# A gated two-layer transformer block on one Trainium2 core: the gathers, the row addition and the order of the last pass

## The reference

```python
def reference(x, ctx_1024, fside, g_xattn, g_ffn, ...):
    x = x + jnp.tanh(g_xattn[0]) * _L0_xattn_ref(_layernorm(x), ctx_1024, ctx_1024, ...)   # mLSTM heads
    x = x + jnp.tanh(g_ffn[0]) * _L0_ffn_ref(_layernorm(x), wg, w1, b1, w2, b2)            # 8 experts
    x = x + jnp.tanh(g_xattn[1]) * _L1_xattn_ref(_layernorm(x), ctx_1024, ctx_1024, fside, W1, b1, W2, b2)
    x = x + jnp.tanh(g_ffn[1]) * _L1_ffn_ref(_layernorm(x), CB, SCB, bias)
    return x

def _L1_xattn_ref(q, k, v1, mask, W1, b1, W2, b2):
    qp = _proj(q, W1, b1, W2, b2)                 # two linear maps
    kp = _proj(k, W1, b1, W2, b2)
    qk = jnp.einsum('bqd,bkd->bqk', qp, kp) * scale + mask
    return jnp.einsum('bqk,bkd->bqd', jax.nn.softmax(qk, axis=-1), v1)

def _L1_ffn_ref(x, CB, SCB, bias):
    return jnp.einsum('bsk,nk->bsn', x, CB) * (SCB * (1.0 / 127.0)) + bias
```

## Time and profile before

| | |
|---|---|
| median of 3 runs | 575.7 us (573.4 to 580.27) |
| profiled execution | 577.31 us, of which the span of the engines' work is 575.5 us |
| last pass in it | first gather at 421.54 us, end at 575.5 us |
| busy share of the span | PE 83%, DVE 58%, ACT 53%, POOL 38% |

### The profile page before, as it was taken

How to read it: one execution, slowest core, us unless ns; L and a number is a source line. 1 busy time by engine, 2 the same in 40 slices (tenths; PEclk the granted TensorE clock), 3 DMA queues, 4 the chain that set the end, 5 groups by cost and what they waited for, 6 DMA issues and landing times. The chain is left out here.

```text
span 575.5 us, 12773 instructions
## 1 busy us (share of the span) xinstructions
PE 478.4 (83%) x3787; PEld 358.4 (62%) x3787; DVE 333.2 (58%) x1455; ACT 306.5 (53%) x764; POOL 217.1 (38%) x210
## 2 busy tenths in 40 slices
PE   3589999999999999964469999999905788888884
PEld 2567787887877778843327777777702455665652
DVE  6335778877778777796322223333213667788772
ACT  4667666656566656331123333333204678888872
POOL 4301124434444435456500000000058888888400
PEclk9997778777787777795569999999965999999997
DMA  4973112222222111141122443343142556666531
GB/s 120 211 197 92 57 57 75 76 75 74 74 75 74 55 54 38 29 122 37 38 55 56 110 111 110 110 109 93 38 113 34 111 109 145 142 137 139 132 93 36
DMA packets 85067, 51.98 MB, mean 90 GB/s; under 512 B 7555, under 2 KB 78886, under 8 KB 85030
## 3 DMA queue, kind: packets, MB, share of 16 engines
q1 hardware_dynamic: 73766, 43.09, 27.3%
q0 software_dynamic: 11264, 8.43, 8.6%
HBM read 26.07 MB, written 16.91 MB: 75 GB/s over the span
## 5 line engine op out<-in xcount | busy, mean ns | idle before, releaser
L684 POOL DMA_INDIRECT s_xs<-slots_y,s_gidx x64 | 98.8, 1544 | 153.8 <-DMA slots_y<-s_ye 134.6
L814 ACT ACTIVATE s_ht<-heads,s_cols 128x512 f32<-128x512 f32 x64 | 44.0, 687 | 85.0 <-PE heads L1061 84.7
L147 ACT ACTIVATE s_xn<-s_xs,s_ln_shift,s_ln_rstd 128x128 f32 (+1 forms) x192 | 77.6, 481 | 15.6 <-DVE s_ln_shift L140 15.5
L662 POOL DMA_INDIRECT slots_x<-s_xn,s_sidx x64 | 62.8, 982 | 22.9 <-issue 22.9
L99 DVE BATCH_NORM_STATS2 s_ln_stats<-s_xs 128x6 f32 (+1 forms) x256 | 54.5, 279 | 25.8 <-DMA s_xs<-slots_y,s_gidx 20.3
L1061 PE MATMUL heads<-s_xet,s_w_sb 128*128 128x512 f32 x128 | 60.2, 615 | 1.7 <-DVE s_xet L1433 1.7
L1068 PE MATMUL bank<-s_w_sb,s_ht 128*128 128x128 f32 x512 | 59.9, 276 | 0.9 <-DVE s_ye L1442 0.9
L1068 PEld LDWEIGHTS bank<-s_w_sb,s_ht 128*128 128x128 f32 x512 | 58.5, 192 | 1.5 <-issue 1.5
L648 POOL TENSOR_TENSOR s_hs<-s_hs,s_head_w 128x512 f32<-128x512 f32 x16 | 20.3, 1268 | 95.0 <-DVE s_hs L1314 94.9
L960 PE MATMUL heads<-s_dec_r,s_dec_l 128*128 128x512 f32 x64 | 50.6, 938 | 2.0 <-DMA s_dec_r<-s_mrow 2.0
L985 PE MATMUL heads<-s_vaug,s_cw 64*64 64x33 f32 x1024 | 50.1, 270 | 0.1
(11 more groups left out here) (190 smaller groups left out, 934.5 us busy)
## 6 DMA issues: line engine op xcount, KB each, us to landing
slots_x<-s_xe SPq DMA_DIRECT2D x8, 516.0 KB, 8.2
s_xe<-slots_x SPq DMA_DIRECT2D x16, 258.0 KB, 3.0
s_xs<-in_x_dram SPq DMA_DIRECT2D x16, 256.0 KB, 3.0
s_ctxb<-in_ctx_dram SPq DMA_DIRECT2D x16, 256.0 KB, 3.2
s_kpt<-s_kt SPq DMA_DIRECT2D x16, 256.0 KB, 2.8
s_w_sb<-in_L_ffn_w_dram SPq DMA_DIRECT2D x16, 256.0 KB, 3.2
slots_y<-s_ye SPq DMA_DIRECT2D x16, 256.0 KB, 2.3
s_ctxv<-in_ctx_dram SPq DMA_DIRECT2D x16, 256.0 KB, 3.7
```

Of the source, the lines that this page charges most:

```text
L147: last = act.activation(out(t), tile(t), ACT.Identity, bias=self.shift[:, j:j + 1], scale=self.rstd[:, j:j + 1])
L662: pool.indirect_dma_start(out=slots_x, out_offset=bass.IndirectOffsetOnAxis(ap=sidx[:, q, t:t + 1], axis=0), in_=xn2[:, q, t, :], in_offse ...
L684: pool.indirect_dma_start(out=xs[:, n * D:(n + 1) * D], out_offset=None, in_=slots_y, in_offset=bass.IndirectOffsetOnAxis(ap=gidx[:, n:n + ...
L814: act.activation(ht[:, s_par, c, :], heads[:, c, :], ACT.Gelu_apprx_tanh, bias=col).then_inc(h_done, 1)
```

## The change

POOL's gathers of the last pass no longer add. Each is a plain indirect transfer into a buffer `yg` of four groups (over the memory of `ex`, which the first pass used). POOL then adds the group to `xs` with one operation of its own, one group behind the gathers. DVE waits for that addition. The gathers wait for the addition of four groups earlier.

The pipeline gets six working stages: first norm (0), queries and scores (1), softmax and values (2), attention added and statistics of the second norm (3), its application (4), last product and output (5). Each engine's order within a step is new. The aggregation of the statistics (`dve_part`) is done directly behind them for each norm. The second norm's aggregation thus lies a step ahead of its use. There are two padding products instead of three. SP starts the loads of keys and of values apart, keys on a wait for scores (`s3_ps`) and six groups ahead of the store, values five groups ahead.

```diff
+    def dve_part(self, dve, i, g, tile):
+        self.dve_stats(dve, i, tile)
+        hold(dve, self.stats_done[i], g + 1, self.go)
+        for t in range(GT):
+            last = dve.bn_aggr(self.mv[:, i * GT + t, :], self.stats[:, i * GT + t, :])
+        last.then_inc(self.part_done[i], 1)
+
+    def dve_variances(self, dve, parts):
+        for i, g in parts:
+            hold(dve, self.part_done[i], g + 1, self.go)
+        c = self.span(parts)
         dve.tensor_scalar(self.ve[:, c], self.mv[:, c, 1], LN_EPS, None, ALU.add).then_inc(self.ve_done, 1)
...
+        yg = ex[:, :, :].rearrange("p q (u t d) -> p (q u) t d", u=2, t=GT)
...
+        KEYS_AHEAD, VALUES_AHEAD = 6, 5
...
+            def load_k(g, q):
+                hold(sp, s3_ps, g - 1, consts)
+                sp.dma_start(kpr[:, q, :], kpt[:, bass.ds(g * GW, GW)]).then_inc(kpr_in[q], 16)
+
+            def load_v(g, q):
                 hold(sp, o3_ps, g - 1, consts)
                 sp.dma_start(ctxv[:, q, :, 0:D], ctx_rows[:, tiles(g), :]).then_inc(v_in[q], 16)
-                sp.dma_start(kpr[:, q, :], kpt[:, bass.ds(g * GW, GW)]).then_inc(kpr_in[q], 16)
...
+            with sp.Fori(0, (NG - KEYS_AHEAD) // 2) as half:
                 for q in range(2):
-                    load_v(half * 2 + q + 3, half + 1 + q, 1 - q)
-                    store(half * 2 + q, half, q)
+                    store(half * 2 + q, q)
+                    load_k(half * 2 + q + KEYS_AHEAD, (q + KEYS_AHEAD) % 2)
+                    load_v(half * 2 + q + VALUES_AHEAD, (q + VALUES_AHEAD) % 2)
...
             def gather(g):
                 if g == 0:
                     pool.wait_ge(read_done, 1)
-                need(pool, ln34.stats_done[0], g - 1)
+                need(pool, y_added, g - 3)
                 for t in range(GT):
                     n = g * GT + t
-                    pool.indirect_dma_start(out=xs[:, n * D:(n + 1) * D], out_offset=None, in_=slots_y,
-                                            in_offset=bass.IndirectOffsetOnAxis(ap=gidx[:, n:n + 1], axis=0),
-                                            compute_op=ALU.add).then_inc(yg_in[g % 2], 16)
-
-            for g in range(NG):
+                    pool.indirect_dma_start(out=yg[:, g % 4, t, :], out_offset=None, in_=slots_y,
+                                            in_offset=bass.IndirectOffsetOnAxis(ap=gidx[:, n:n + 1], axis=0)).then_inc(yg_in[g % 2], 16)
+
+            def add_rows(g):
+                pool.wait_ge(yg_in[g % 2], g // 2 * (16 * GT) + 16 * GT)
+                pool.tensor_tensor(xgroup(g), xgroup(g), yg[:, g % 4, :, :].rearrange("p t d -> p (t d)"),
+                                   ALU.add).then_inc(y_added, 1)
+
+            gather(0)
+            for g in range(1, NG):
                 gather(g)
+                add_rows(g - 1)
+            add_rows(NG - 1)
...
@@ scalar, last_pass: the order of a step @@
-                if four: turned_probabilities(*four)
-                if norms: ln34.act_guess(act, k, norms)
-                if three: projected_queries(*three)
-                if five: ln34.act_apply(...)          # second norm
-                if two: ln34.act_apply(...)           # first norm
+                if two: probabilities(*two)
+                if one: queries3(*one)
+                if norms: ln34.act_guess(act, k, norms)
                 if five: rows4(*five)
-                if three: probabilities(*three)
-                if two: queries3(*two)
+                if two: turned_probabilities(*two)
+                if one: projected_queries(*one)
+                if zero: ln34.act_apply(...)          # first norm
+                if four: ln34.act_apply(...)          # second norm
...
             def turn_rows4(g, half, q):
                 need(pe, xt4_done, g)
-                keep_clock(6, 3)
+                keep_clock(6, 2)
...
@@ tensor, last_pass: the order of a step @@
-                if four: turn_probabilities(*four)
-                if three: project_queries(*three)
-                if four: values3(*four)
-                if three: scores3(*three)
+                if one: turn_queries3(*one)
                 if five: turn_rows4(*five)
-                if two: turn_queries3(*two)
+                if two: turn_probabilities(*two)
+                if one: project_queries(*one)
                 if five: product4(*five)
+                if one: scores3(*one)
+                if two: values3(*two)
...
@@ vector, last_pass @@
+                if two:
+                    score_maxima(*two)
+                if zero:
+                    hold(dve, y_added, zero[0] + 1, consts)
+                    ln34.dve_part(dve, 0, zero[0], xtile(zero[0]))
                 if norms:
-                    k = step_of(at[1:5])
-                    ln34.dve_moments(dve, k, norms)
-                if six:
-                    outputs(*six)
+                    k = step_of(at)
+                    ln34.dve_variances(dve, norms)
+                if three:
+                    attention_sums(*three)
+                    add_attention(*three)
                 if norms:
                     ln34.dve_newton(dve, k, norms)
                     ln34.dve_shift(dve, k, norms)
-                if four:
-                    attention_sums(*four)
                 if three:
-                    score_maxima(*three)
-                if four:
-                    add_attention(*four)
+                    hold(dve, x3_done, three[0] + 1, consts)
+                    ln34.dve_part(dve, 1, three[0], xtile(three[0]))
+                if five:
+                    outputs(*five)
```

More of the change, by code:

```diff
@@ L82, in __init__ @@
         self.mv_done = sem(f"{name}_mv_done")
+        self.part_done = [sem(f"{name}_part_done{i}") for i in range(2)]
         self.ve_done = sem(f"{name}_ve_done")
@@ L111, in dve_moments @@
         dve.wait_ge(self.mv_done, k + 1)
+        dve.tensor_scalar(self.ve[:, c], self.mv[:, c, 1], LN_EPS, None, ALU.add).then_inc(self.ve_done, 1)
+    def dve_part(self, dve, i, g, tile):
[8 more added lines that the diff above has]
+        c = self.span(parts)
         dve.tensor_scalar(self.ve[:, c], self.mv[:, c, 1], LN_EPS, None, ALU.add).then_inc(self.ve_done, 1)
@@ L573, in _ @@
                 sp.wait_ge(keys_kept[q], 16 * NG // 2)
[L574 to L577, removed]
-                for q in range(2):
-                    load_v(half * 2 + q + 3, half + 1 + q, 1 - q)
-                    store(half * 2 + q, half, q)
[L581 to L584, removed]
+            load_k(0, 0)
+            load_k(1, 1)
+            load_v(0, 0)
+            load_v(1, 1)
+            for g in range(2, KEYS_AHEAD):
+                load_k(g, g % 2)
+                if g < VALUES_AHEAD:
+                    load_v(g, g % 2)
+            with sp.Fori(0, (NG - KEYS_AHEAD) // 2) as half:
+                for q in range(2):
+                    store(half * 2 + q, q)
+                    load_k(half * 2 + q + KEYS_AHEAD, (q + KEYS_AHEAD) % 2)
+                    load_v(half * 2 + q + VALUES_AHEAD, (q + VALUES_AHEAD) % 2)
+            for g in range(NG - KEYS_AHEAD, NG):
+                store(g, g % 2)
+                if g + VALUES_AHEAD < NG:
+                    load_v(g + VALUES_AHEAD, (g + VALUES_AHEAD) % 2)
             for q in range(2):
@@ L854, in last_pass @@
             def last_pass(at):
-                one, two, three, four, five = at
-                norms = [(i,) for i, here in enumerate((two, five)) if here]
-                if four:
-                    turned_probabilities(*four)
+                zero, one, two, _, four, five = at
+                norms = [(i,) for i, here in enumerate((zero, four)) if here]
+                if two:
+                    probabilities(*two)
+                if one:
+                    queries3(*one)
                 if norms:
-                    k = step_of(at[1:])
+                    k = step_of(at)
                     ln34.act_guess(act, k, norms)
[L862 to L869, removed]
                 if five:
                     rows4(*five)
-                if three:
-                    probabilities(*three)
                 if two:
-                    queries3(*two)
+                    turned_probabilities(*two)
+                if one:
+                    projected_queries(*one)
+                if zero:
+                    need(act, q3_ps, zero[0])
+                    ln34.act_apply(act, k, 0, lambda t: xn3[:, t, :], xtile(zero[0]))
+                if four:
+                    need(act, xt4_ps, four[0])
+                    ln34.act_apply(act, k, 1, lambda t: xn4[:, t, :], xtile(four[0]))
             act.preload_act_table_set("natural_log_exp_and_others")
-            over_groups(act, NG, 5, last_pass)
+            over_groups(act, NG, 6, last_pass)
         @block.tensor
@@ L1162, in last_pass @@
             def last_pass(at):
-                one, two, three, four, five = at
-                if four:
```

(20 more changed lines are left out.)

20 lines of the change are left out of this document (6 added, 14 removed).

## The result

The changed kernel takes 572.84 us at the median against 577.87 us for the kernel before on the same chip (20 runs each). The ratio is 0.9925 with a 95% interval of 0.9901 to 0.9948, a gain of about 4.3 us by that ratio (the two medians alone differ by 5.0). The forecast was a gain of 8. The profiled execution has a span of 570.2 us against 575.5.

What follows compares the result with a forecast made beforehand. POOL's queue (7.40 us a group) and a similar chain bound the last pass; POOL at 6.85 brings group 15's statistics from 543.4 to 535.4, 8.0 us less, drain equal: between 569.3 and 567.7, forecast 568.5 us, range 562 to 578.

Steps and rivals of the forecast that it cites:

- What bounds the kernel before: Last pass: POOL's queue at 7.40 us a group, beside a chain round PE, DVE and ACT at about the same.
- The price of the plain gather: POOL, last pass: 0.97 us per plain gather, taken from the first pass's plain scatter, instead of 1.54 for the adding gather.
- POOL's pace: Last pass: four plain gathers, idle times and one addition make 6.85 us a group on POOL.
- So POOL paces the steps: Last pass: POOL's 6.85 us exceeds the chain's 6.6, so the other engines follow with little to spare.
- if POOL stops long before DVE gets to its groups: Stated sign of being wrong, last pass: POOL finishing far ahead would mean that the chain paces.
- So they miss each other: Last pass: DVE's refinements miss POOL's next addition by 1.9 us, as long as DVE follows POOL directly.
- The rival: Last pass: POOL's additions hold DVE's refinements, DVE up to 3.9 us behind, pace not slowed; 572.4 us, chance 0.10.
- the rule: SBUF port pair shared by two-input DVE instructions and POOL: second starter blocks; alone, over a microsecond lost per step.
- The chain: Last pass: the cycle through DVE, ACT and PE takes 13.2 us over two steps, 6.6 us a step.
- The drain: End of the last pass: 29.2 us from group 15's statistics to the last output's end, equal to before.
- The loads: SP's separate key and value loads: issued a full step ahead, cover 6.8 us, effect put at nothing.
- The clock rival: PE in the fill: clock stays longer at 1.2 GHz, costing 10 to 13 us, giving 580 us; chance 0.07.

Runs made afterwards that it cites:

- second experiment: Changed kernel with one more wait: POOL's addition of a group starts only after DVE's shift of the step before; 565.85 us, ratio 0.981 to the kernel before.
- seventh experiment: Changed kernel with a 128x640 memset on POOL behind each addition, slowing POOL to 6.74 us a group; 568.18 us, ratio 0.9809 to the kernel before.
- second measurement: The changed kernel measured once more, with nothing changed; 572.60 us, ratio 0.9906 to the kernel before.

## Why the prediction was wrong

- **What bounds the kernel before: right.** POOL's queue and the chain stood side by side at 7.4 us. Either one alone gives nothing: 0.997 for the order, 1.012 for the gathers.
- **The price of the plain gather: right.** 0.97 forecast, 0.948 measured; the addition 1.29 against 1.28. Its wait for gathers cost nothing in the loop, as forecast (one wait in all, 0.8 us), though the scatters of the earlier trace rows land after up to 3.1 us and not "within 2.3 us".
- **POOL's pace: the step that failed.** "4 x 0.97 + 3 x 0.30 + 0.52 + 0.26 + 1.29 = 6.85 us" is 4 x 0.948 + 3 x 0.30 + 0.16 + 0.01 + 1.28 = 6.14, and 6.17 from addition to addition in the timeline. The two idle times were taken from places of the first pass with other neighbours: the 0.52 stands behind a cast, the 0.26 between two dependent operations. Each was sized from above, and 0.6 us of caution turned the order of the two paces around. "So POOL paces the steps" was wrong: POOL leads, and the chain paces. The prediction had named this as a sign of being wrong ("if POOL stops long before DVE gets to its groups").
- **"So they miss each other" falls with it.** That rested on DVE's statistics starting when the addition ends. It was so in two steps. After that the additions of 6.16 us drift through steps of 6.84 and hit whatever stands there. Seen from the first gather, the statistics of group 15 would have come after 110.0 us without holds (second experiment), 3.9 better than forecast (in the fill DVE's statistics still come about 6.2 us apart, POOL's pace). They came after 118.0. The holds cost about 8.0 us, the forecast 113.9 was missed by 4.1.
- **The rival named the right cause with a wrong bound.** Of contention it says that "it keeps DVE up to 3.9 us behind" and "can't slow the pace". It does. An addition holds DVE up to 1.8 us and POOL doesn't wait for DVE in return, so nearly every step pays. The rival's 572.4 lies beside the measured 572.8 by chance.
- **The Trainium skill** (SBUF — State Buffer, "Who interferes with whom") lists both kinds: VectorE instructions with two SBUF inputs, and `tensor_scalar`, which can enter a mode with two ports. I used the first half of the rule only. The trace shows both, line 142 at 1.84 and line 128 at 1.47 us. The runs show that overlap with the addition causes the holds. That a port is the reason is what the skill states, and no run here tells it from another shared part. "Whichever starts second blocks" isn't what the rows show: both instructions start ahead of POOL's addition (473.68 against 474.20, 480.21 against 480.36) and are held all the same.
- **The chain: right in size.** 6.6 forecast; 6.84 in the loop without holds, 6.25 to 6.40 without the loop. Two of its terms, 4.0 and 1.5 us on PE, had no row behind them, and only their sum is tested by the steps. The drain was right too, 28.1 against 29.2.
- **The loads: right for the change, incomplete as a reading.** Nobody waits for keys or values in the changed kernel, but it lives on a lead of one step that the old program would not have had.
- **The clock rival: did not come.** The granted clock is 1.00 between 454 and 539 us, as before.

## What to carry to other kernels

An engine that runs ahead is not free: where it shares something with the engine that sets the pace, its slack can turn into hits on that engine. Here one wait that ties its long operation to a stretch in which the other isn't held by it cured that. When two forecast paces are close (here 6.85 and 6.6), take the idle times from both sides as well and ask what happens if their order turns around.

## What the runs showed of the hardware

- Beside a POOL addition of 128x512, DVE's small instructions of 0.16 us last up to 1.95 us, with one SBUF input (TENSOR_SCALAR) or two. The BATCH_NORM_STATS, maxima, attention and output rows beside it kept their durations (0.28, 0.42, 0.34, 0.69 us). A POOL memset of 128x640 held a TENSOR_SCALAR of 128x4 too (0.55 us, seventh experiment).
- The hold can be longer than POOL's row: line 142 starts at 473.68, POOL's addition at 474.20, and both end together. In the changed kernel and its second measurement held instructions start up to 0.64 us ahead of POOL's row. POOL may have the port that much before its row starts; no run settles that.
- An indirect gather of 128 rows of 512 bytes keeps POOL for 0.948 us, with addition on the way for 1.54.
- A loop of two steps took 6.84 us a step, the same code written out 6.40 (ratios 0.981 and 0.971).
